# One matmul over 128 columns in place of two over 64, in the products of a linear attention layer

## The chip, the cores and the metric

The kernel runs on one core of one Trainium2 chip. The metric is the device time of one execution in microseconds (us), the median of several runs.

## The reference, cut to what matters

The reference is one transformer block over T = 4096 tokens of width 256. A layer norm (scaled and shifted) feeds a gated delta-rule attention with H = 8 heads and M = 8 modes of memory per head; then a second layer norm feeds a mixture of 8 experts, of which each token takes two. Everything is float32. The attention is the long part, and in it each of the 64 pairs of head and mode carries a 64x64 memory S through the tokens:

```python
def step(S, inp):
    q_t, k_t, v_t, b_g, b_beta = inp
    S = S * jnp.exp(b_g)[..., None, None]
    kv = jnp.einsum('mbhk,mbhkv->mbhv', k_t, S)
    dv = (v_t[None] - kv) * b_beta[..., None]
    S = S + k_t[..., :, None] * dv[..., None, :]
    o_t = jnp.einsum('mbhk,mbhkv->mbhv', q_t, S)
    return (S, o_t)
S0 = jnp.zeros((M, B, H, DK, DV), jnp.float32)
_, ys = jax.lax.scan(step, S0, (qt, kt, vt, gt, bt))
```

Queries and keys are rotated by an angle that depends on the mode, and brought to unit length, before this.

## The kernel before, in words

**Tiles and chunks.** The tokens are cut into 32 tiles of 128, a tile into NC = 4 chunks of C = 32 tokens. The 64 pairs of head and mode are taken in two halves of 32 (hh = 0 and 1), a half as HQ = 8 quads q of four modes of one head; the 128 partitions hold four modes x 32. Within a chunk the recurrence is solved in closed form: Gram products of keys with keys and queries, a 32x32 triangular system for each pair (the solve), and then, chunk after chunk, a read of the memories, corrections, and an update of the memories.

**The four products that the edit touches**, all on TensorE (PE), all f32, with 128 rows and a stationary operand of 128 columns that is cut into SIDES, columns 0 to 63 and 64 to 127, each in a matmul of its own that writes 64 partitions of the result:
- gram(u, c), L518: keys `ke` against keys and queries `kq`, 64 moving columns, for 8 quads and r = 0, 1 (the halves of the key's 64 dimensions).
- memory_read(v, hh, c), L557: `ke` against `state`, 64 moving columns, 8 quads x 2, in two groups g of four quads, each with a semaphore of its own.
- corrections(v, hh, c), L574: `te` (the inverse) against `rhs`, 64 moving columns, 8 quads, in two groups; behind each group stand the half-width products of L580 (`state` against the queries `qg`), which write outputs to 64 partitions at a time.
- update_and_outputs(v, c), L593: `kte` against `dvs`, 64 moving columns, 8 quads x 2, in two groups; behind each stand the half-width products of L601.

The stationary operands `ke`, `te` and `kte` are block-diagonal, with 32x32 blocks for the four modes of a quad; ScalarE (ACT) copies the blocks into place (L751, L758, L793).

**Order.** The order is written out by hand, for each engine in a function half(n, hh), and the engines meet at counting semaphores. In half(n, hh) each engine does the front of its own half u = 2n + hh and, in between, the four chunks of the half before, v = u - 1. On PE: read, corrections, update of chunk 0; read of chunk 1, rows (L493), corrections, update; replicate (L502), read of chunk 2, replicate, corrections, update; rows, read of chunk 3, corrections, gram 0, rows, update of chunk 3, gram 1, 2, 3; then project_out (even halves, L610), values (L529), the next tile's projections (L467), route (even halves, L618 and L623), sum_squares (L475). The read of the next chunk 0 stands at the head of the next half, behind columns (L483) in the even ones, and so runs during the solve.

On VectorE (DVE): right_sides (L1237, L1240) takes a read and makes `rhs`; decayed_corrections (L1247) takes the corrections and makes `dvs`; update_memories (L1256, L1258) adds the update to the state and takes the outputs. Between them stand the front's operations (angles, L1119 to L1127; decays, L1144 to L1148; rotate_keys, L1163 to L1173; chunk_systems, L1205 and L1206, which take a Gram product each; queries_for_memories, L1197). At the end comes the solve, L1210 to L1224, some 31 pairs of short operations, without PE. GpSimd (POOL) fades the state (L1527) between corrections and update, and rotates the queries.

In each group PE waits for DVE's result and DVE for PE's, as here:

```python
pe.wait_ge(sem(f"state_ready{g}"), since(f"state_ready{g}", vc))
pe.wait_ge(sem(f"dv_ready{g}"), since(f"dv_ready{g}", vc))
pe.wait_ge(sem(f"out_taken{g}"), since(f"out_taken{g}", vc))
```

Gram products, rows and key replicas go through two PSUM banks in turn (to_dve); PE waits for a bank to be freed.

Of the kernel before, what the change touches and what calls it, by code (L numbers as in the profile page):

```python
# [21 lines left out]
P = 128  # L22
# [3 lines left out]
H, M, DK = 8, 8, 64  # L26
FR = DK // 2
C = 32
# [3 lines left out]
HQ = Q // 2  # L32
# [87 lines left out]
def build(nc, x_in, Wq, Wk, Wv, Wbeta, Wtg, mode_logits, log_decay, omega_log, Wg, Wo,  # L120
# [11 lines left out]
    with outer, ctx:  # L132
# [35 lines left out]
        def sb(name, shape, dt=F32):  # L168
            return ctx.enter_context(nc.sbuf_tensor(name, shape, dt))
# [6 lines left out]
        bank_mem = banks[4:6]  # L176
        bank_upd = banks[6:8]
# [70 lines left out]
        dvs = sb("dvs", [P, HQ, DK])  # L248
# [5 lines left out]
        kq = sb("kq", [P, 2, HQ, 2, P])  # L254
        ke = sb("ke", [P, NC, 2, HQ, P])
        kte = sb("kte", [P, 2, HQ, P])
        te = sb("te", [P, HQ, P])
# [6 lines left out]
        state = sb("state", [P, Q, 2, DK])  # L264
        rhs = sb("rhs", [P, HQ, DK])
# [148 lines left out]
        def _(pe):  # L414
# [92 lines left out]
            SIDES = (slice(0, 64), slice(64, 128))  # L507

            def gram(u, c):

                pe.wait_ge(sem("q_rotated"), since("q_rotated", u + 1))
                pe.wait_ge(sem("ke_ready"), 4 * u + c + 1)

                def emit(b):
                    for q in range(HQ):
                        for r in range(2):
                            for s in SIDES:
                                mm = pe.matmul(b[s, q * 2 * C:(q + 1) * 2 * C], ke[:, c, r, q, s],  # L518
                                               kq[:, r, q, :, c * C:c * C + C], start=(r == 0), stop=(r == 1))
                    return mm  # L520
                to_dve(emit)

# [24 lines left out]
            def memory_read(v, hh, c):  # L547

                vc = 4 * v + c
                for g in range(2):  # L550
                    pe.wait_ge(sem(f"state_ready{g}"), since(f"state_ready{g}", vc))
                    pe.wait_ge(sem(f"dv_ready{g}"), since(f"dv_ready{g}", vc))
                    pe.wait_ge(sem(f"out_taken{g}"), since(f"out_taken{g}", vc))
                    for q in range(4 * g, 4 * g + 4):
                        for r in range(2):
                            for s in SIDES:
                                mm = pe.matmul(bank_mem[g][s, q % 4 * DK:q % 4 * DK + DK], ke[:, c, r, q, s],  # L557
                                               state[:, hh * HQ + q, r, :], start=(r == 0), stop=(r == 1))
                    mm.then_inc(sem(f"ks_full{g}"), 1)

            def out_bank(g, side):
# [3 lines left out]
            def corrections(v, hh, c):  # L565

                vc = 4 * v + c
                for g in range(2):
                    pe.wait_ge(sem(f"rhs_ready{g}"), since(f"rhs_ready{g}", vc + 1))  # L570
                    pe.wait_ge(sem("te_ready"), vc + 1)
                    for q in range(4 * g, 4 * g + 4):
                        for s in SIDES:
                            pe.matmul(bank_mem[g][s, q % 4 * DK:q % 4 * DK + DK], te[:, q, s], rhs[:, q, :], start=True, stop=True)  # L574
                    pe.wait_ge(sem("qg_ready"), v + 1)
                    for j in range(2):
                        for r in range(2):
                            for side in range(2):
                                q = 4 * g + 2 * side + j
                                mm = pe.matmul(out_bank(g, side), state[:, hh * HQ + q, r, :], qg[:, r, q, c * C:c * C + C],  # L580
                                               start=(j == 0 and r == 0), stop=False)
                    mm.then_inc(sem(f"dv_full{g}"), 1)

            def update_and_outputs(v, c):

                vc = 4 * v + c
                for g in range(2):
                    pe.wait_ge(sem(f"dvs_ready{g}"), since(f"dvs_ready{g}", vc + 1))
                    pe.wait_ge(sem("kte_ready"), vc + 1)
                    for q in range(4 * g, 4 * g + 4):  # L590
                        for r in range(2):
                            for s in SIDES:
                                mm = pe.matmul(bank_upd[g][s, (q % 4) * P + r * DK:(q % 4) * P + r * DK + DK],  # L593
                                               kte[:, r, q, s], dvs[:, q, :], start=True, stop=True)
                    mm.then_inc(sem(f"upd_full{g}"), 1)
                    pe.wait_ge(sem(f"dv_ready{g}"), since(f"dv_ready{g}", vc + 1))
                    pe.wait_ge(sem("pw_ready"), since("pw_ready", v + 1))
                    for j in range(2):
                        for side in range(2):
                            q = 4 * g + 2 * side + j  # L600
                            mm = pe.matmul(out_bank(g, side), dv[:, q, :], pw[:, c, q, :], start=False, stop=(j == 1))  # L601
                    mm.then_inc(sem(f"out_full{g}"), 1)
# [1207 lines left out]
```

## Time and profile before

| | |
|---|---|
| time, median of 3 runs | 7432.92 us (7431.34 to 7433.24) |
| the profiled execution's own time | 7433.18 us |
| its span, first to last instruction | 7431.5 us |
| mean granted TensorE clock | 0.803 |
| busy: PE, PEld, DVE, ACT, POOL | 61%, 53%, 77%, 44%, 44% of the span |

Busy time is the time in which an engine had at least one instruction under way. PE is the matmul side of TensorE, PEld its weight loads, which overlap it.
### The profile page before, as it was taken

What the parts mean: (1) busy time and instruction counts of PE and PEld (TensorE: products, weight loads), DVE (VectorE), ACT (ScalarE), POOL (GpSimd) and SP (SyncE); (2) the same over time, 40 slices, a digit from 0 to 9 for tenths busy, and PEclk for the clock granted to TensorE, in tenths of its full rate; (3) what the DMA queues carried; (4) which work ended last, traced back from release to release, by engine and by line L of the source; (5) the groups of instructions that cost most, each with busy time, mean ns of one, the idle gap of its engine ahead of it and who ended that gap; (6) DMA issues with size and microseconds to landing.
All of it is one profiled execution on the core that took longest, in us unless ns stands there. A gap on an engine that the chain in (4) does not pass through costs nothing. (4 is left out here: it accounts for less than half of the span.)

```text
span 7431.5 us, 196282 instructions
## 1 busy us (share of the span) xinstructions
PE 4567.1 (61%) x78513; PEld 3915.4 (53%) x78513; DVE 5741.0 (77%) x10216; ACT 3284.2 (44%) x5497; POOL 3289.4 (44%) x2021
## 2 busy tenths in 40 slices
PE   1565656656666666566565666666665656663994
PEld 0455555555555555555555555555555555553662
DVE  5788888888888888888888888888888888883003
ACT  0444445444445444454444544444444445452220
POOL 0545454454454454544545544445445455453003
PEclk9787778877778777787777887777877778876997
DMA  2000000000000000000000000000000000003223
GB/s 80 1 5 5 5 5 5 3 4 5 5 5 5 5 5 5 5 5 2 5 5 5 5 5 5 5 5 5 5 2 5 5 5 5 5 4 108 68 71 99
DMA packets 68598, 107.85 MB, mean 15 GB/s; under 512 B 11824, under 2 KB 57200, under 8 KB 66544
## 3 DMA queue, kind: packets, MB, share of 16 engines
q1 hardware_dynamic: 59248, 69.78, 2.9%
q0 software_dynamic: 8448, 25.18, 1.1%
q8 instruction: 672, 11.01, 0.6%
q14 instruction: 230, 1.88, 0.1%
HBM read 57.32 MB, written 37.62 MB: 13 GB/s over the span
## 5 line engine op out<-in xcount | busy, mean ns | idle before, releaser
L1527 POOL TENSOR_TENSOR state<-state,gc_end 128x512 f32<-128x512 f32 x512 | 594.9, 1174 | 1359.2 <-PE bank L580 1319.0
L574 PE MATMUL bank<-rhs,te 128*64 128x64 f32 x8192 | 451.8, 270 | 887.4 <-DVE rhs L1240 551.3
L574 PEld LDWEIGHTS bank<-rhs,te 128*64 128x64 f32 x8192 | 378.1, 177 | 974.1 <-DVE rhs L1240 925.5
L557 PE MATMUL bank<-state,ke 128*64 128x64 f32 x16384 | 660.3, 249 | 319.3 <-DVE outT L1258 232.2
L557 PEld LDWEIGHTS bank<-state,ke 128*64 128x64 f32 x16384 | 620.9, 161 | 439.9 <-DVE state L1256 247.7
L751 ACT ACTIVATE te<-tt 32x256 f32<-32x256 f32 x1024 | 421.9, 412 | 742.8 <-DVE tt L1224 732.3
L593 PE MATMUL last_two<-dvs,kte 128*64 128x64 f32 x16384 | 638.2, 236 | 180.5 <-DVE dvs L1247 180.5
L1221 DVE TENSOR_TENSOR last_two<-last_two,prod 128x31 f32<-128x31 f32 (+15 forms) x1984 | 692.6, 349 | 68.1
L793 ACT ACTIVATE ke<-kq 32x512 f32<-32x512 f32 x1024 | 642.7, 628 | 201.7 <-DVE kq L1173 188.0
L1219 DVE TENSOR_TENSOR prod<-bd,last_two 128x31 f32<-128x31 f32 (+15 forms) x1984 | 671.1, 338 | 71.9
L593 PEld LDWEIGHTS last_two<-dvs,kte 128*64 128x64 f32 x16384 | 575.3, 149 | 196.7 <-DVE dvs L1247 187.7
L758 ACT ACTIVATE kte<-kt 32x512 f32<-32x512 f32 x1024 | 641.5, 626 | 34.4 <-PE last_two L593 21.2
L518 PE MATMUL bank<-kq,ke 128*64 128x64 f32 x16384 | 581.1, 237 | 114.4 <-DVE pw L1206 105.8
L1552 POOL TENSOR_TENSOR pw<-pw,w_quad 128x1024 f32<-128x1024 f32 x64 | 122.4, 1913 | 1176.1 <-DVEq L1398 1176.1
L518 PEld LDWEIGHTS bank<-kq,ke 128*64 128x64 f32 x16384 | 561.5, 152 | 122.6 <-DVE pw L1206 74.7
L1489 POOL TENSOR_TENSOR kq<-tmp,turn 128x1024 f32<-128x1024 f32 x320 | 607.1, 1897 | 32.0 <-POOL pw L1552 5.6
L766 ACT ACTIVATE dv<-bank 128x256 f32<-128x256 f32 x512 | 188.4, 380 | 743.0 <-DVE dvs L1247 733.5
L493 PE MATMUL bank<-row_group,select 128*128 128x128 f32 x3072 | 426.9, 293 | 36.2 <-DVE col L1136 27.6
L1256 DVE TENSOR_TENSOR state<-last_two,state 128x512 f32<-128x512 f32 x512 | 354.0, 691 | 117.4 <-POOL state L1527 77.8
L1722 DVE TENSOR_TENSOR yrow<-last_two,b_row 128x256 f32<-128x256 f32 x64 | 27.2, 425 | 504.5 <-PE last_two L1676 504.5
L493 PEld LDWEIGHTS bank<-row_group,select 128*128 128x128 f32 x3072 | 384.2, 201 | 55.1 <-DVE col L1136 27.9
L1540 POOL TENSOR_TENSOR tmp<-raw,cos_t 128x1024 f32<-128x1024 f32 x64 | 151.8, 2371 | 588.8 <-ACTq L834 588.8
(248 smaller groups left out, 11015.0 us busy)
## 6 DMA issues: line engine op xcount, KB each, us to landing
w_sb<-in_L_ffn_W_dram SPq DMA_DIRECT2D x16, 1024.0 KB, 9.3
expert_rows<-ke SPq DMA_DIRECT2D x1, 8192.0 KB, 21.3
xrows<-expert_rows SPq DMA_DIRECT2D x16, 512.0 KB, 8.3
expert_outputs<-yrow POOLq DMA_DIRECT2D x16, 512.0 KB, 3.4
xt<-_attn_hidden_states_dram SPq DMA_DIRECT2D x32, 128.0 KB, 2.1
xr<-_attn_hidden_states_dram SPq DMA_DIRECT2D x32, 128.0 KB, 2.1
x_after_attention<-xr SPq DMA_DIRECT2D x32, 128.0 KB, 1.7
xo<-x_after_attention SPq DMA_DIRECT2D x32, 128.0 KB, 3.7
```

Source lines behind the costliest of these rows:

```text
L493: mm = pe.matmul(b[:, ql * P:ql * P + P], select[:, b4 * 4 + ql, :], row_group[:, group, :], start=True, stop=True)
L518: mm = pe.matmul(b[s, q * 2 * C:(q + 1) * 2 * C], ke[:, c, r, q, s], kq[:, r, q, :, c * C:c * C + C], start=(r == 0), stop=(r == 1))
L557: mm = pe.matmul(bank_mem[g][s, q % 4 * DK:q % 4 * DK + DK], ke[:, c, r, q, s], state[:, hh * HQ + q, r, :], start=(r == 0), stop=(r == 1))
L574: pe.matmul(bank_mem[g][s, q % 4 * DK:q % 4 * DK + DK], te[:, q, s], rhs[:, q, :], start=True, stop=True)
L593: mm = pe.matmul(bank_upd[g][s, (q % 4) * P + r * DK:(q % 4) * P + r * DK + DK], kte[:, r, q, s], dvs[:, q, :], start=True, stop=True)
L751: ins = act.activation(te[s, :, 32 * m:32 * m + 32], tt[s, c, :, :], ACT.Copy)
L758: ins = act.activation(kte[s, :, :, 32 * m:32 * m + 32].rearrange("p r q f -> p (r q) f"), kt[s, :, :, c * C:c * C + C].rearrange("p r q f ...
L793: ins = act.activation(ke[s, c, :, :, 32 * m:32 * m + 32].rearrange("p r q j -> p (r q) j"), kq[s, :, :, 0, c * C:c * C + C].rearrange("p ...
L1219: ln(dve.tensor_tensor(pr, a_prob[:, j + 1:C, j:j + 1].broadcast_to([P, rows, cols]), t_prob[:, j:j + 1, 0:cols].broadcast_to([P, rows, co ...
L1221: ln(dve.tensor_tensor(below, below, pr, ALU.subtract))
L1489: ln(pool.tensor_tensor(low2 if i else into, part, over_t(table), ALU.mult))
L1527: pool.tensor_tensor(sv, sv, gc_end[:, vh, 4 * g:4 * g + 4, c].unsqueeze(2).broadcast_to([P, 4, 2 * DK]), ALU.mult).then_inc(sem(f"state_f ...
```

## The change

In the four products the loop over SIDES goes, and one matmul takes all 128 stationary columns and writes all 128 partitions of the result. The moving operand, the order, the waits and the semaphores stay. The products of L580 and L601 stay as they are, 64 columns at a time.

```diff
                 def emit(b):
                     for q in range(HQ):
                         for r in range(2):
-                            for s in SIDES:
-                                mm = pe.matmul(b[s, q * 2 * C:(q + 1) * 2 * C], ke[:, c, r, q, s],
-                                               kq[:, r, q, :, c * C:c * C + C], start=(r == 0), stop=(r == 1))
+                            mm = pe.matmul(b[:, q * 2 * C:(q + 1) * 2 * C], ke[:, c, r, q, :],
+                                           kq[:, r, q, :, c * C:c * C + C], start=(r == 0), stop=(r == 1))
...
                         for r in range(2):
-                            for s in SIDES:
-                                mm = pe.matmul(bank_mem[g][s, q % 4 * DK:q % 4 * DK + DK], ke[:, c, r, q, s],
-                                               state[:, hh * HQ + q, r, :], start=(r == 0), stop=(r == 1))
+                            mm = pe.matmul(bank_mem[g][:, q % 4 * DK:q % 4 * DK + DK], ke[:, c, r, q, :],
+                                           state[:, hh * HQ + q, r, :], start=(r == 0), stop=(r == 1))
...
                     for q in range(4 * g, 4 * g + 4):
-                        for s in SIDES:
-                            pe.matmul(bank_mem[g][s, q % 4 * DK:q % 4 * DK + DK], te[:, q, s], rhs[:, q, :], start=True, stop=True)
+                        pe.matmul(bank_mem[g][:, q % 4 * DK:q % 4 * DK + DK], te[:, q, :], rhs[:, q, :], start=True, stop=True)
...
                         for r in range(2):
-                            for s in SIDES:
-                                mm = pe.matmul(bank_upd[g][s, (q % 4) * P + r * DK:(q % 4) * P + r * DK + DK],
-                                               kte[:, r, q, s], dvs[:, q, :], start=True, stop=True)
+                            mm = pe.matmul(bank_upd[g][:, (q % 4) * P + r * DK:(q % 4) * P + r * DK + DK],
+                                           kte[:, r, q, :], dvs[:, q, :], start=True, stop=True)
```

## Rows read from the trace of the kernel before

**Rows 1.** Page: busy share of each engine, and PE's granted clock in 40 slices.
```profile
PE 4567.1 (61%) x78513; PEld 3915.4 (53%) x78513; DVE 5741.0 (77%) x10216; ACT 3284.2 (44%) x5497; POOL 3289.4 (44%) x2021
...
PEclk9787778877778777787777887777877778876997
```

**Rows 2.** Windows: stretch, length, busy us of each engine, PEclk, DMA share, GB/s.
```profile
3055.00:3059.70 4.70, 2.85 (x54) 2.88 (x56) 4.04 (x7) 1.77 (x5) 0.74 (x1) 0.50 0.02 3
3059.70:3069.00 9.30, 7.08 (x179) 6.77 (x179) 7.86 (x13) 6.79 (x12) 1.36 (x2) 0.99 0.01 2
...
3055.00:3154.50 99.50, 63.29 (x1208) 55.53 (x1208) 83.44 (x152) 50.11 (x85) 47.80 (x26) 0.81 0.03 7
3154.50:3259.80 105.30, 64.57 (x1192) 57.00 (x1192) 89.62 (x156) 48.68 (x82) 50.31 (x32) 0.78 0.01 2
```

**Rows 3.** Timeline, PE: start, us, line, shape, records, idle before and its releaser.
```profile
3041.53 1.92 PE L483 MATMUL bank<-cmat,xg 128*128 128x32 f32 x8 [9.18 <-DVE xg L1090]
3043.37 3.34 PE L557 MATMUL bank<-state,ke 128*64 128x64 f32 x64
3056.85 1.12 PE L574 MATMUL bank<-rhs,te 128*64 128x64 f32 x16 [10.14 <-ACT te L751]
3057.73 1.05 PE L580 MATMUL bank<-qg,state 128*64 128x32 f32 x16
3058.55 1.13 PE L574 MATMUL bank<-rhs,te 128*64 128x64 f32 x16
...
3064.79 2.10 PE L557 MATMUL bank<-state,ke 128*64 128x64 f32 x64 [2.22 <-DVE outT L1258]
3066.82 2.05 PE L493 MATMUL bank<-row_group,select 128*128 128x128 f32 x16
3068.85 0.69 PE L574 MATMUL bank<-rhs,te 128*64 128x64 f32 x16
...
3069.81 0.66 PE L574 MATMUL bank<-rhs,te 128*64 128x64 f32 x16
...
3070.74 1.13 PE L593 MATMUL last_two<-dvs,kte 128*64 128x64 f32 x32
3071.80 0.42 PE L601 MATMUL bank<-pw,dv 128*64 128x32 f32 x8
...
3101.79 3.15 PE L518 MATMUL bank<-kq,ke 128*64 128x64 f32 x64
...
3124.57 1.95 PE L467 MATMUL bank<-hT,wqk_sb 128*128 128x128 f32 x16
3126.36 0.27 PE L618 MATMUL bank<-cmat,xn 128*128 128x128 f32 x1
...
3128.47 0.61 PE L623 MATMUL bank<-wr_sb,h2T 128*128 128x8 f32 x4 [0.93 <-ACTq L883]
```

**Rows 4.** Timeline, DVE, in the same columns.
```profile
3018.32 0.17 DVE L1077 RECIPROCAL stat<-stat 128x1 f32<-128x1 f32 x1 [2.22 <-ACT stat L773]
...
3071.03 0.42 DVE L1247 TENSOR_TENSOR dvs<-bank,dec_end 128x256 f32<-128x256 f32 x1 [0.51 <-PE bank L580]
...
3078.80 0.42 DVE L1237 TENSOR_TENSOR rhs<-bank,eg_col 128x256 f32<-128x256 f32 x1
...
3079.88 1.23 DVE L1163 TENSOR_TENSOR tmp<-bank,cos_t 128x1024 f32<-128x1024 f32 x1 [0.19 <-DVE rhs L1240]
...
3091.60 0.69 DVE L1256 TENSOR_TENSOR state<-last_two,state 128x512 f32<-128x512 f32 x1 [1.04 <-POOL state L1527]
...
3104.99 0.42 DVE L1205 TENSOR_TENSOR cos_t<-bank,bd 128x256 f32<-128x256 f32 x1 [1.40 <-PE bank L518]
...
3119.84 0.42 DVE L1206 TENSOR_TENSOR pw<-bank,dec 128x256 f32<-128x256 f32 x1
```

**Rows 5.** Groups by line: shape, records, busy us, mean ns, idle before, releasers.
```profile
L557 PE MATMUL bank<-state,ke 128*64 128x64 f32 x16384 | 660.3, 249 | 319.3 <-DVE outT L1258 232.2 <-issue 87.1
...
L574 PE MATMUL bank<-rhs,te 128*64 128x64 f32 x8192 | 451.8, 270 | 887.4 <-DVE rhs L1240 551.3 <-ACT te L751 336.0
```

## The prediction

> **What bounds the kernel now.** I read the page's busy shares first, then the windows with the granted clock, then the timelines of PE and DVE over one half tile side by side, and the groups by line last, for counts. The page says DVE 77% and PE 61% busy [rows 1], which reads as a DVE-bound kernel with room on PE. The windows keep that picture and give the period: a pair of halves takes 99.5 + 105.3 = 204.8 us, with PE busy 63 to 65 us and DVE 83 to 90 us of each half [rows 2]. The timelines correct it. From the end of the solve (3055) to the last Gram product (3120) DVE and PE work in a ring: DVE waits for each read, correction, update and Gram product, and PE waits for the DVE operation between them [rows 3, 4]. From 3064.8 to 3073 PE runs without a gap: read of chunk 1, rows, corrections, update. There every added PE microsecond lands on the path. The solve, where PE idles ten microseconds on end (ahead of 3056.85), hides what is added there (the read of chunk 0).
>
> **Price of one record.** An f32 matmul is two records here: 16,384 records at L557 are 8,192 half matmuls [rows 5]. So are they at L518 and L593, and 8,192 records at L574 are 4,096. The edit turns 57,344 half-width records into 28,672 full-width ones, 448 for each half tile (read 128, corrections 64, update 128, Gram 128). Full clock, half width: 64 records of L557 start at 3064.79 and the next line at 3066.82, 0.032 us each, 0.062 to 0.064 a pair (16 of L574 in 0.52 give 0.065) [rows 3]. Full clock, full width: 16 records of L467 (128 moving columns) take 1.79, 0.112 each. With fewer moving columns it gets no cheaper: the four of L623 stream 8 columns and take 0.61 in all; less the length of a single one (0.27, the L618 row) that is 0.34 for three starts, 0.113. So a full-width record costs what its 128 stationary columns cost, and 64 moving columns stream under it. Half clock: L483 (32 moving columns, full width) takes 1.84 for 8 with one turn behind, 0.215 each; a pair of halves takes 2 x 0.055 = 0.11 (16 of L574 in 0.88) [rows 3]. A merged record thus costs 0.112 in place of 0.063, or 0.215 in place of 0.11. Bounds where no row shows 64 columns on 128: below, the stream alone, half of L467's 0.112 = 0.056; above, 0.127 (16 of L493 in 2.03). I take 0.112, since 8 and 128 columns cost the same.
>
> The Trainium skill, page "TensorE: Matmul & The Clock Gate", speaks for both. Its section "Back-to-back issue gap" gives about 60 cycles for anything up to 64 moving columns; by that a merged record would take about 0.025 to 0.05 us and PE would get lighter. Its section "LDWEIGHTS (loading the stationary operand)" has the time go by stationary columns, 128 / 1.2 GHz, an estimate of 0.107. The L623 row sides with the second.
>
> **Turns.** The output products of L580 and L601 stay half width, so PE now turns between full and half width inside every chunk: eight times. The 16 records of L493 take 2.03 where 16 x 0.112 = 1.79, with a turn on either side: about 0.1 us a turn, between 0 and 0.24 [rows 3].
>
> **New stage costs, full clock.** Read of a chunk: 32 x 0.112 = 3.6 for 2.0. Corrections: a group takes 0.96 (3068.85 to 3069.81); its 16 half records (0.5) become 8 x 0.112 = 0.9 and two turns 0.2, so 1.55, twice. Update: a group of 32 half records (1.06, from 3070.74 to 3071.80) and 8 of L601 at 0.03 becomes 1.8 + 0.2 + 0.2 = 2.2, twice. Gram: 3.6 for 2.0. Removing instructions frees nothing else: PE's queue order, all waits and all DMAs stay.
>
> **The clock.** The half starts with PE at half clock after ten idle microseconds (3055 to 3059.7 at 0.50), and it rises at 3059.8, after 3 us of closely packed half-width work [rows 2, 3]. With merged records at half clock the same columns stream over twice the time (0.215 for 0.11), so the array is half as densely fed. The L483 work, thin and full width, ran at the half clock throughout. I therefore take it that the clock stays low through chunk 0 and the read of chunk 1 and rises only in the rows products of L493, whose 128 moving columns feed the array fully. Once up I let it stay up while PE is not kept waiting, as in 3059.7 to 3069 (0.99). No row here shows a packed but thin burst, so that the clock rises as early as now is the first rival. The Trainium skill, page "TensorE: Matmul & The Clock Gate", section "What's actually happening", ties the clock to how busy PE has been; a merged burst has no gaps, so that reading speaks for this rival.
>
> **The sum along one half** (times of the half that starts at 3055; delay against it) [rows 3, 4].
> Chunk 0 at half clock: corrections 2 x (8 x 0.215 + 0.82 for L580 + 0.24) = 5.5 from 3056.85, to 3062.3; update 2 x (3.4 + 0.34 + 0.24) = 8.0, to 3070.3; read of chunk 1, 32 x 0.215 = 6.9, to 3077.2; rows, mostly at half clock, 3.1, to 3080.3. Corrections of chunk 1 began at 3068.85: +11.5. DVE's work in between (add, columns, state, sin_t, unit: about 7 us) lies beside this.
> Chunk 1 at full clock: corrections +1.1, so DVE's second dvs (3071.03) is 12.5 late; update +1.8, read of chunk 2 +1.5, with a few tenths of turns: the rhs of 3078.80 is +15.4.
> Chunk 2: the update was waited for by nobody: DVE rotates keys from 3079.9 on and then waits for POOL's fade at 3091.60. Eight microseconds of update, if the 2 us gap ahead of it drops the clock again, just fit beneath: 0 (at most 1.2).
> Chunk 3: that update runs from 3100.6 to 3108.0, the rows behind it to 3111.1, the read to 3114.7. Its second rhs is then ready at 3115.9, 0.5 more than 15.4 late; the second group of corrections ends at 3117.8 and the first Gram product (3101.79 now) at 3121.3. DVE, which waits 1.40 for it at 3104.99, takes it at 3121.6: +16.6.
> Update of chunk 3 and Gram products 1 to 3: DVE had 2.0 us of its own work between products that took 2.0; now they take 3.6, PE sets the pace, and the last product (3119.84) is +19.0.
> Behind it, project_out is late by 0.7 in the even halves; in the odd ones ACT's square root is queued behind the values products, and DVE's wait of 2.22 for it (3018.32) grows by 2.5.
> That is 19.7 + 21.5 = 41.2 us a tile. There are 63 halves with memories, 31.5 tiles: 1,298. The four chunks after the last half have no rows products among them and run at half clock: by the same prices about 30 (10 to 60). The first half adds 3. Together 1,330 on the profiled execution's own 7433.18 (span 7431.5; the median of the runs is 7432.92, so the two need no correction): 8,760.
>
> **Rivals.**
> First, the clock rises as early as now. Then chunk 0 costs 0.9, the read 1.6 and the corrections 1.1, less 0.4 of turns that the rows no longer need: +3.2 at 3071.03. Update and read make +6.3 at 3078.80, the first Gram product +6.8 at 3104.99, update and three Gram products +9.2 at 3119.84. With the same two extras as above that is 9.9 and 11.7 a half, 21.6 x 31.5 + 15 = 695: 8,130. For it: PE is packed in chunk 0 as before. Against: the thin stream at half clock, above. Chance 0.20.
> Second, the clock stays low for longer: the rows products don't lift it, and chunk 1 and the first Gram product run at half clock too: corrections 5.5 for 3.1, update 8.0 for 4.4, read 6.9 for 3.6, Gram 6.9 for 3.6, some 12.6 more a half, about 9,550. Against: those rows products stream twice the columns per record. Chance 0.08.
> Third, on the other side: the stationary load hides behind the stream, the lower bound of 0.056 holds. Then a half's 448 records save 448 x (0.063 - 0.056) = 3 us, and some 21 more turns at 0.1 cost 2: no change, 7,420 to 7,445. It decides in favour of the change only if a turn is free, too. The one thing for it is that no row has 64 moving columns on 128; L623 speaks against it. Chance 0.05, in equal parts above and below the mark.
> Fourth, that the added PE time vanishes in PE's 36 us of idle a half (7,433). That idle is in one long gap in the solve and in gaps at which PE waits for a DVE result that itself waits for PE. I give it 0.01.
>
> **How the numbers follow.** My forecast has 0.66; its own range, from the turn (0 to 0.24), the update of chunk 2 (0 to 1.2) and the point in the rows where the clock rises (plus or minus 2 us a half), is 8,600 to 8,920. To hold 8 in 10 the range takes in the first rival: 8,100 to 9,000. About 0.2% is what a measurement tells from no change here; slower by more than that 0.94, within it 0.03, faster 0.03.
>
> **What would show it.** In the profile after: records of L518, L557, L574 and L593 halved, start to start 0.11 at full clock (0.056 would make the third rival right); the window from the end of the solve to the read of chunk 1 at a granted clock near 0.5 (near 1.0 from 5 us on is the first rival); DVE's idle time ahead of L1237, L1247, L1256 and L1205 grown to some 20 us a half; a pair of halves near 246 us, DVE's busy time unchanged. A pair under 210 us would make the forecast wrong at its root.

## The result, and the profile after: slower by a fifth

The median after is 8904.3 us (8895.3 to 8907.9, 4 runs) against 7432.8 (7431.3 to 7433.2, 4 runs): a ratio of 1.198, 95% interval [1.196, 1.200], or +1,471 us. The prediction was 8,760 in a range of 8,100 to 9,000, so direction and mechanism held, and the growth of 1,330 was 140 us (10%) short; two larger errors lie beneath it and partly cancel, as the part on the prediction shows. Lines behind the change moved up by four, so that L1247 of before is L1243 of after; the merged products are L517 (Gram), L555 (read), L571 (corrections) and L589 (update), and the half-width ones L577 and L597. In the experiments further on the lines shift again by a few, and the names of the tiles tell which product a row is.

The page of the kernel after, busy us of each engine and the granted clock in 40 slices:

```profile
PE 7003.8 (79%) x49841; PEld 6362.6 (71%) x49841; DVE 5544.0 (62%) x10216; ACT 3299.5 (37%) x5497; POOL 3270.1 (37%) x2021
...
PEclk9677777777777777777777777777777777776797
```

Against [rows 1] PE has 28,672 fewer records, as counted, and 2,437 us more of busy time; the mean granted clock fell from 0.803 to 0.748. The half tile that stood at 3055 in [rows 2 to 4] stands at 3666.5 now (subtract 611.5 to compare). Windows of it, in the columns of [rows 2]:

```profile
3666.66:3671.20 4.54, 2.82 (x24) 2.72 (x24) 3.62 (x6) 1.54 (x4) 0.00 (x0) 0.50 0.00 0
3671.20:3683.00 11.80, 11.80 (x79) 11.21 (x75) 5.33 (x9) 3.37 (x8) 2.10 (x2) 0.50 0.00 0
3683.00:3689.90 6.90, 6.90 (x33) 6.90 (x34) 2.98 (x6) 6.00 (x7) 0.00 (x0) 0.50 0.01 2
3689.90:3705.50 15.60, 14.83 (x135) 13.09 (x133) 6.27 (x14) 4.81 (x10) 2.10 (x2) 0.90 0.01 1
...
3713.70:3729.80 16.10, 16.10 (x96) 15.74 (x96) 9.59 (x13) 9.81 (x18) 13.83 (x7) 0.58 0.01 2
3729.80:3743.30 13.50, 13.47 (x148) 12.85 (x146) 8.87 (x15) 5.79 (x10) 2.10 (x2) 1.00 0.00 1
```

PE is busy without a gap from 3671.2 to 3689.9, and its clock stays at the lower level (0.50) all that time, where before it rose after 4.7 us [rows 2]. The timeline of PE, in the columns of [rows 3]:

```profile
3668.38 1.94 PE L571 MATMUL bank<-rhs,te 128*128 128x64 f32 x8 [6.52 <-ACT te L747]
...
3674.15 3.68 PE L589 MATMUL last_two<-dvs,kte 128*128 128x64 f32 x16
...
3682.51 7.09 PE L555 MATMUL bank<-state,ke 128*128 128x64 f32 x32
3689.39 3.73 PE L493 MATMUL bank<-row_group,select 128*128 128x128 f32 x16
3692.91 1.05 PE L571 MATMUL bank<-rhs,te 128*128 128x64 f32 x8
...
3713.70 3.68 PE L589 MATMUL last_two<-dvs,kte 128*128 128x64 f32 x16 [1.67 <-DVE dvs L1243]
...
3722.06 3.78 PE L493 MATMUL bank<-row_group,select 128*128 128x128 f32 x16
3725.64 4.40 PE L555 MATMUL bank<-state,ke 128*128 128x64 f32 x32
...
3733.07 3.79 PE L517 MATMUL bank<-kq,ke 128*128 128x64 f32 x32
```

Start to start, a full-width record takes 0.213 us at half clock (the median of such distances; 32 of L555, and the next line starts 6.88 later) and 0.112 at full (32 of L517, next start at 3736.70). The rows products at 3689.39 still take 3.52 to the next start, so the clock rose only at their end; by the trace's clock records it did so at 3693.0. DVE on the other side of the ring:

```profile
3674.34 0.42 DVE L1243 TENSOR_TENSOR dvs<-bank,dec_end 128x256 f32<-128x256 f32 x1 [2.54 <-PE bank L577]
...
3682.10 0.69 DVE L1252 TENSOR_TENSOR state<-last_two,state 128x512 f32<-128x512 f32 x1 [3.26 <-PE last_two L589]
...
3689.71 0.42 DVE L1233 TENSOR_TENSOR rhs<-bank,eg_col 128x256 f32<-128x256 f32 x1 [2.60 <-PE bank L555]
...
3696.29 0.42 DVE L1243 TENSOR_TENSOR dvs<-bank,dec_end 128x256 f32<-128x256 f32 x1 [1.20 <-PE bank L577]
...
3707.32 0.42 DVE L1233 TENSOR_TENSOR rhs<-bank,eg_col 128x256 f32<-128x256 f32 x1 [0.97 <-PE bank L555]
...
3724.18 0.69 DVE L1177 TENSOR_TENSOR bd<-bank,dec 128x512 f32<-128x512 f32 x1 [0.98 <-PE bank L493]
...
3736.90 0.42 DVE L1201 TENSOR_TENSOR cos_t<-bank,bd 128x256 f32<-128x256 f32 x1 [2.29 <-PE bank L517]
...
3754.72 0.42 DVE L1202 TENSOR_TENSOR pw<-bank,dec 128x256 f32<-128x256 f32 x1
```

Every wait in these rows names PE, with a product of the ring behind it. Summed over the kernel, DVE's groups by line show where the time sits. First the kernel before, then after; the last figures are the idle time ahead of the group:

```profile
L1237 DVE TENSOR_TENSOR rhs<-bank,eg_col 128x256 f32<-128x256 f32 x512 | 217.4, 425 | 202.8 <-issue 98.5 <-PE bank L557 69.5 <-DVE tt L1224 1.0
L1247 DVE TENSOR_TENSOR dvs<-bank,dec_end 128x256 f32<-128x256 f32 x512 | 217.3, 424 | 113.1 <-PE bank L580 96.7
L1256 DVE TENSOR_TENSOR state<-last_two,state 128x512 f32<-128x512 f32 x512 | 354.0, 691 | 117.4 <-POOL state L1527 77.8 <-DVE qg L1198 14.4 <-DVE tmp L1124 6.8
L1205 DVE TENSOR_TENSOR cos_t<-bank,bd 128x256 f32<-128x256 f32 x256 | 108.7, 425 | 111.9 <-PE bank L518 89.0
L1181 DVE TENSOR_TENSOR bd<-bank,dec 128x512 f32<-128x512 f32 x128 | 88.5, 691 | 15.4
```

```profile
L1233 DVE TENSOR_TENSOR rhs<-bank,eg_col 128x256 f32<-128x256 f32 x512 | 217.3, 424 | 635.1 <-PE bank L555 528.8 <-issue 98.7 <-DVE tt L1220 1.0
L1243 DVE TENSOR_TENSOR dvs<-bank,dec_end 128x256 f32<-128x256 f32 x512 | 217.2, 424 | 550.1 <-PE bank L577 537.7
L1252 DVE TENSOR_TENSOR state<-last_two,state 128x512 f32<-128x512 f32 x512 | 353.9, 691 | 564.8 <-PE last_two L589 485.1 <-POOL state L1523 65.5 <-DVE qg L1194 14.2
L1201 DVE TENSOR_TENSOR cos_t<-bank,bd 128x256 f32<-128x256 f32 x256 | 108.7, 425 | 270.7 <-PE bank L517 266.9
L1177 DVE TENSOR_TENSOR bd<-bank,dec 128x512 f32<-128x512 f32 x128 | 88.5, 692 | 99.8 <-PE bank L493 99.7
```

The idle time ahead of these five grew by 432 + 437 + 447 + 159 + 84 = 1,560 us. DVE's own busy time fell by 197 (5741.0 to 5544.0), so that 1,363 of the 1,471 stand in these rows; 86 more are the odd halves' wait for ACT's square root (2.8 a half), and 24 the even halves' wait for project_out.

### The profile page after: what moved, and what is told of

The parts are those of the page before. It is cut to its first block and busy times, and to the rows that moved or that the text cites. A ratio compares the mean times of both kernels' runs of the same rounds, so it can differ in the third digit from the quotient of the medians.

```text
span 8901.4 us, 138938 instructions
## 1 busy us (share of the span) xinstructions
PE 7003.8 (79%) x49841; PEld 6362.6 (71%) x49841; DVE 5544.0 (62%) x10216; ACT 3299.5 (37%) x5497; POOL 3270.1 (37%) x2021
## 5 line engine op out<-in xcount | busy, mean ns | idle before, releaser
L589 PE MATMUL last_two<-dvs,kte 128*128 128x64 f32 x8192 | 1444.5, 350 | 110.8 <-DVE dvs L1243 110.8
L555 PEld LDWEIGHTS bank<-state,ke 128*128 128x128 f32 x8192 | 1381.2, 266 | 142.5 <-issue 138.2
L589 PEld LDWEIGHTS last_two<-dvs,kte 128*128 128x128 f32 x8192 | 1367.8, 261 | 138.3 <-DVE dvs L1243 118.0
L555 PE MATMUL bank<-state,ke 128*128 128x64 f32 x8192 | 1397.3, 351 | 59.7 <-issue 59.7
L571 PE MATMUL bank<-rhs,te 128*128 128x64 f32 x4096 | 683.2, 322 | 502.7 <-DVE rhs L1236 284.1
L571 PEld LDWEIGHTS bank<-rhs,te 128*128 128x128 f32 x4096 | 632.3, 234 | 555.9 <-DVE rhs L1236 513.5
L517 PE MATMUL bank<-kq,ke 128*128 128x64 f32 x8192 | 945.5, 276 | 7.7 <-POOL kq L1543 7.7
L517 PEld LDWEIGHTS bank<-kq,ke 128*128 128x128 f32 x8192 | 927.9, 192 | 13.5 <-POOL kq L1543 8.0
L1233 DVE TENSOR_TENSOR rhs<-bank,eg_col 128x256 f32<-128x256 f32 x512 | 217.3, 424 | 635.1 <-PE bank L555 528.8
L1243 DVE TENSOR_TENSOR dvs<-bank,dec_end 128x256 f32<-128x256 f32 x512 | 217.2, 424 | 550.1 <-PE bank L577 537.7
```

Source lines behind the costliest of these rows:

```text
L517: mm = pe.matmul(b[:, q * 2 * C:(q + 1) * 2 * C], ke[:, c, r, q, :], kq[:, r, q, :, c * C:c * C + C], start=(r == 0), stop=(r == 1))
L555: mm = pe.matmul(bank_mem[g][:, q % 4 * DK:q % 4 * DK + DK], ke[:, c, r, q, :], state[:, hh * HQ + q, r, :], start=(r == 0), stop=(r == 1))
L571: pe.matmul(bank_mem[g][:, q % 4 * DK:q % 4 * DK + DK], te[:, q, :], rhs[:, q, :], start=True, stop=True)
L589: mm = pe.matmul(bank_upd[g][:, (q % 4) * P + r * DK:(q % 4) * P + r * DK + DK], kte[:, r, q, :], dvs[:, q, :], start=True, stop=True)
```

## The experiments

### One of the four products at a time

Each run takes one of the four hunks of the change and leaves the other three products in halves.

```diff
 e1_gram_only   +  mm = pe.matmul(b[:, ...], ke[:, c, r, q, :], kq[...], ...)
 e2_read_only   +  mm = pe.matmul(bank_mem[g][:, ...], ke[:, c, r, q, :], state[...], ...)
 e3_corr_only   +  pe.matmul(bank_mem[g][:, ...], te[:, q, :], rhs[:, q, :], ...)
 e4_upd_only    +  mm = pe.matmul(bank_upd[g][:, ...], kte[:, r, q, :], dvs[:, q, :], ...)
```

Gram products: 

> Only the Gram products (L518) are merged to 128 columns; reads, corrections and updates stay in halves. Theory (a full-width record costs what its 128 stationary columns cost, and a thin merged burst does not lift the clock): the first Gram product starts at half clock now (3101.79), so it costs 6.8 for 2.9 us and the rows behind it some 1 more; products 1 to 3 cost 2.4 behind the update; with project_out and ACT's square root some 1.6: about 8.5 us a half, 7,900 to 8,000 us. Rival, that only the price of the record counts and the clock goes as before: 1.6 + 2.4 + 1.6 = 5.6 a half, about 7,790. Rival, that the load hides behind the stream: 7,430.

Read: 

> Only the reads (L557) are merged. Theory: reads of chunks 1 and 2 cost 1.6 each at full clock and land on the path, the read of chunk 3 falls partly at half clock and is partly covered by DVE, the read of chunk 0 lies in the solve: 3 to 4.5 us a half, 7,620 to 7,720 us. Rival, that the load hides behind the stream: 7,430.

Corrections: 

> Only the corrections (L574) are merged, which brings a turn to and from half width around each group. Theory: +1.2 us a chunk at full clock and some 2 at half clock; chunk 2 is covered by DVE's rotation; the clock rises one step later in chunk 0: about 4 us a half, 7,630 to 7,730 us. If a turn costs nothing: 2.5 us a half, about 7,590. Rival, that the load hides behind the stream and only the turns are left: about 7,460.

Update: 

> Only the updates (L593) are merged. Theory: +1.8 to 2 us in each of chunks 0, 1 and 3 at full clock, more where the burst meets the half clock (odd halves, chunk 0), chunk 2 mostly covered: 5.5 to 8 us a half, 7,780 to 7,930 us. The four parts then add up to about the 1,471 us of the whole; a sum well below it would say that the merged kernel pays for something that no part alone brings (the longer stretch at half clock). Rival, that the load hides behind the stream: 7,440.

| alone | median us | ratio to before | growth |
|---|---|---|---|
| Gram | 7869.5 | 1.059 [1.057, 1.061] | 437 |
| read | 7808.7 | 1.051 [1.050, 1.053] | 376 |
| corrections | 7754.8 | 1.044 [1.042, 1.045] | 322 |
| update | 7755.3 | 1.044 [1.042, 1.045] | 322 |

No part is free, and together they make 1,457, which is the whole within 1%. That sum is no proof that the parts are independent: the update alone takes 71 us off DVE's wait for the Gram products (111.9 before, 40.8 then). In size all four expectations were off, Gram and update below their range, read and corrections above. For Gram, the first product of a half meets half clock and a waiting DVE:

```profile
2960.28 7.09 PE L517 MATMUL bank<-kq,ke 128*128 128x64 f32 x32
...
2967.41 0.42 DVE L1204 TENSOR_TENSOR cos_t<-bank,bd 128x256 f32<-128x256 f32 x1 [5.46 <-PE bank L517]
```

```profile
L1204 DVE TENSOR_TENSOR cos_t<-bank,bd 128x256 f32<-128x256 f32 x256 | 108.7, 425 | 442.1 <-PE bank L517 434.2
```

That wait was 1.40 [rows 4], so 4.1 us a half (3.9 expected), or some 260 us. Over the kernel DVE's idle time ahead of all four Gram products grew by 330 us (442.1 for 111.9), which leaves some 70 for products 1 to 3, 1.1 a half for the 2.4 expected. The rows that the queries wait for add 52, the square root in the odd halves (5.01 for 2.22 in [rows 4]) 86 and project_out 24, all near what was expected; and DVE's own busy time fell by 59. So Gram came under its range by products 1 to 3 and by DVE's shorter operations.

Update alone, DVE's idle time ahead of the state additions grew by 320 us and ahead of bd by 84; 71 less at the Gram products and 89 less of busy time gave part of it back. Corrections alone, the waits grew by 2.3 us a half in chunk 0, 1.3 in chunk 1 and 1.4 ahead of the Gram products, each a little over its price. The read shows a cost of another kind. The read of chunk 1 stands behind a gap (2.10 here), and in 47 of 63 halves the clock falls within it, although the corrections and updates before it are still in halves (4.66 us to the next start here, 3.59 in the other halves). It takes the rows products behind it along:

```profile
3001.46 4.86 PE L556 MATMUL bank<-state,ke 128*128 128x64 f32 x32 [2.10 <-DVE outT L1257]
3006.12 3.73 PE L493 MATMUL bank<-row_group,select 128*128 128x128 f32 x16
```

DVE then waited 4.11 us for the corrections (0.38 before), and 1.85 in the halves in which the clock stayed up. So the price of a merged product includes the clock of work behind it that the change doesn't touch.

### The price of a record, by itself

Blocks of matmuls on constants, placed ahead of the first tile, each on a line of its own; the rest is the kernel before. It leaves nothing out.

```diff
+            for _ in range(60):
+                pe.matmul(bank_mem[1][:, 0:64], ident, cmat[:, 0:64], start=True, stop=True)
+            for _ in range(100):
+                for s in SIDES:
+                    pe.matmul(bank_mem[1][s, 0:64], ident[:, s], cmat[:, 0:64], start=True, stop=True)
...
```

> The kernel before with ten blocks of matmuls of constants put ahead of its first tile, one line each, so its time is not compared. Full width with 64 moving columns (60 matmuls), half-width pairs of 64 (100), full width 64 (120), full width 32 (80), 128 (60), 256 (60), pairs of 32 (80), full 128 (60), full 8 (60), full 128 (30). Theory: start to start of a full-width record is 0.112 us at full clock and 0.213 at half for 8, 32, 64 and 128 moving columns alike, 0.216 for 256; a pair of half-width records of 64 is 0.06. The first block, thin and packed, leaves the clock at half although PE never pauses; the pairs lift it; the second block of 64 keeps it; the block of 32 loses it. Rival on the clock (it goes by packed or not): the first block lifts it within a few us and nothing loses it. Rival on the price: 64 and 32 moving columns cost 0.056 and less.

The timeline of PE over the blocks:

```profile
153.68 25.83 PE L435 MATMUL bank<-cmat 128*128 128x64 f32 x120 [116.37 <-POOLq L1483]
179.44 13.35 PE L438 MATMUL bank<-cmat 128*64 128x64 f32 x400
192.72 27.01 PE L440 MATMUL bank<-cmat 128*128 128x64 f32 x240
219.57 30.54 PE L442 MATMUL bank<-cmat 128*128 128x32 f32 x160
...
265.53 26.07 PE L446 MATMUL bank<-cmat 128*128 128x256 f32 x120
291.53 9.53 PE L449 MATMUL bank<-cmat 128*64 128x32 f32 x320
300.98 13.66 PE L451 MATMUL bank<-cmat 128*128 128x128 f32 x120
314.49 21.27 PE L453 MATMUL bank<-cmat 128*128 128x8 f32 x120
```

Three things can be read. First, 240 full-width records with 64 moving columns take 26.85 us to the next start, 0.112 each; with 128 columns it is 0.113 (L451), and with 8 columns (L453) the records stand 0.112 apart as well, until the clock falls in it, too. Only with 256 does the stream show (0.216). A half-width record takes a quarter of 0.112: once L438 is at full clock its records stand 29 ns apart on average, 58 ns a pair, and with 32 moving columns (L449) it is 30 ns. So the price goes by the stationary side up to 128 moving columns, and two stationary operands of 64 columns side by side cost half of one of 128. (Two on the same side in a row were not run.) The prediction's third rival needed 0.056 for the merged record.

The Trainium skill's page "TensorE: Matmul & The Clock Gate" has in its section "Back-to-back issue gap" a table with some 60 cycles for up to 64 moving columns. The table is for an isolated matmul, and the section says that in a stream of weight loads and matmuls both set the spacing; the 0.112 of this stream agrees with the text and not with the table. The section "LDWEIGHTS (loading the stationary operand)" takes columns / 1.2 ns, which makes an estimate of 107 ns for 128 columns, near the 112 measured at full clock. It makes 53 ns for 64 columns, where this stream has 29, and it doesn't tell the two levels of the clock apart, where this stream has 213 at the lower one.

Second, PE has no gap in L435 and yet its records stand 0.215 us apart for 25.8 us, the price at half clock. The trace has no clock record ahead of the first rise, which comes 3.3 us into the half-width pairs of L438, so the view prints 1.00 for this stretch and the half clock is inferred from the distances; a DMA load of 205 GB/s runs beside L435, too, and it is the less clean of the two witnesses. Third, a thin stream even loses the clock. The window in L442, whose records have 32 moving columns:

```profile
223.70:249.90 26.20, 26.20 (x125) 26.20 (x125) 0.00 (x0) 0.00 (x0) 0.00 (x0) 0.50 0.00 1
```

PE is busy for 26.20 of 26.20 us and its clock is at the lower level. With 64 columns (L440) it kept the upper level; L435 did not reach it. The same page of the Trainium skill, section "What's actually happening", lets the clock follow how busy PE has been; by busy time as the profile counts it this window should have kept the clock, and it didn't.

### How much of the loss is clock

First, chunk 0 and the read of chunk 1 go back to halves, and all else stays merged:

```diff
+                            for s in (SIDES if c == 1 else (slice(0, P),)):    # read
...
+                        for s in (SIDES if c == 0 else (slice(0, P),)):        # corrections, update
```

> The changed kernel with the corrections and update of chunk 0 and the read of chunk 1 in halves again, three of its fifteen stages. Theory: the clock rises in chunk 0 as in the kernel before, and the 13.7 us by which DVE is late at the corrections of chunk 1 shrink to about 2 (rows and corrections): 11 to 12 us a half, about 8,180 us. Rival (only the price at full clock counts): the three stages give back 0.9 + 1.6 and little more, about 3 us a half, 8,710.

Measured: 8189.3 us, ratio 1.102 [1.100, 1.104]. With 80 of a half's 448 merged records (corrections 16, update 32, read 32) split again, 715 of 1,471 us are gone. At the record's full-clock price they would be 80 x 0.05 = 4 us a half, some 250, and six turns fewer at 0.1 some 40; the rest is the clock, which rises in chunk 0 again.

Second, the records stay merged, and PE gets full matmuls of 512 moving columns, their result unused, in its idle time ahead of the corrections of chunk 0:

```diff
+            def fill(n):
+                if n:
+                    b = to_scalar.bank()
+                    pe.wait_ge(sem(f"act_bank_free{b}"), since(f"act_bank_free{b}", to_scalar.uses_of_bank()))
+                    for _ in range(n):
+                        pe.matmul(bank_act[b][:, :], ident, cmat[:, 0:512], start=True, stop=True)
...
                     memory_read(v, vh, 0)
+                    fill(5 if hh == 0 else 8)
                     corrections(v, vh, 0)
```

> The changed kernel with full-width matmuls of constants, 512 moving columns each, put into PE's gap between the read of chunk 0 and its corrections (5 in the even halves, 8 in the odd ones; results are not used). No stage of the change is touched; only PE's clock at the start of the ring differs. Theory: corrections 3.2 for 5.8, update 4.6 for 8.4, read 3.6 for 6.9, rows 1.8 for 3.5, that is 11.4 us of PE, of which about 10.5 reach the path: 63 x 10.5 = 660, about 8,240 us. If the clock has no part in it: 8,904 or more.

Measured: 8280.0 us (8250.2 to 8367.1), 1.117 [1.111, 1.123]: 624 us less for added work. In the profiled execution the clock fell again in chunk 0 in 11 of the 32 odd halves, which then took 126.8 us in place of 117.5 or 119.3; so the 624 are what these fillers gave, not the whole of what the clock costs. Then one matmul more, ahead of the update of chunk 2, which in the kernel after starts behind a wait of 1.67 and runs at half clock:

```diff
                     corrections(v, vh, 2)
+                    fill(1)
                     update_and_outputs(v, 2)
```

> The changed kernel with the filler of chunk 0 and one filler more ahead of the update of chunk 2, PE's next gap (1.67 us). Theory: that update, the rows behind it and the start of the read of chunk 3 come at full clock, and DVE's waits there (0.8 for the update, 1.0 and 1.0 for rows, 1.7 and 1.0 for the read) mostly go: 4 to 5 us a half, about 8,000 us. What then is left over 7,433 is the price at full clock, 9 us a half. If the clock costs nothing there: 8,280.

A miss: 8680.5 us (8665.7 to 8684.6), 1.168 [1.166, 1.170], 400 us worse than without it. It did what it was put there for: the update of chunk 2 and the read of chunk 3 ran at full clock. But the fall only came later, in the thin, waiting work of chunk 3, where the first Gram product sits:

```profile
3262.57 1.10 PE L579 MATMUL bank<-rhs,te 128*128 128x64 f32 x8 [1.14 <-DVE rhs L1246]
...
3265.06 1.97 PE L579 MATMUL bank<-rhs,te 128*128 128x64 f32 x8 [0.80 <-DVE rhs L1246]
...
3267.96 7.09 PE L525 MATMUL bank<-kq,ke 128*128 128x64 f32 x32
```

The half lengths became 122 in place of 108.6 in the even halves and 120 to 121 in place of 117.5 to 126.8 in the odd ones. The last experiment takes that up, with fillers at every thin place (6 and 10 at chunk 0, and two each ahead of the update of chunk 2, the read and the corrections of chunk 3):

```diff
+                    fill(6 if hh == 0 else 10)
                     corrections(v, vh, 0)
...
+                    fill(2)
                     update_and_outputs(v, 2)
                 rows(2 + hh)
                 if not first:
+                    fill(2)
                     memory_read(v, vh, 3)
+                    fill(2)
                     corrections(v, vh, 3)
```

> The changed kernel with extra full matmuls (512 moving columns, result unused) ahead of the corrections of chunk 0 (6 and 10 a half), and two each ahead of the update of chunk 2, the read of chunk 3 and its corrections, where one filler at chunk 2 alone had only moved the place at which the clock falls. If what is left beyond the merged records' own price is the clock, and thin stages need company at every gap, then all stages run at full clock: the price is that of the prediction's first rival, 21.6 us a tile or some 680 us, on the 7,381 of the unchanged kernel with the same fillers: 8,030 to 8,150, halves of some 105 and 117, the first Gram product streaming 32 records in 3.8. If the thin full-width stages lose the clock whatever stands between them, 8,300 to 8,700 as in the two versions with fewer fillers, with updates of 3.68 a group in chunk 2 or a Gram 0 of 7.09.

Measured: 8119.6 us (8117.7 to 8121.9), 1.092 [1.091, 1.094], halves of 108.1 and 117.2. Of the 8,192 full-width records each of the update and of Gram products, 2% at most ran at half clock; what else did is the read of chunk 0, beneath the solve. The page's clock slices, and the read of chunk 1 and Gram product 0 that took 7.09 in the kernels above:

```profile
PEclk9798888988889888898888998889888899886997
```

```profile
3007.83 3.79 PE L563 MATMUL bank<-state,ke 128*128 128x64 f32 x32
...
3050.64 3.79 PE L525 MATMUL bank<-kq,ke 128*128 128x64 f32 x32
```

So of the 1,471 us, 785 go away when fillers hold the clock, and 687 are what the merged records and turns cost at full clock (with what the fillers cost or give themselves). The split depends on what it is measured against: the kernel before gains 52 us by fillers in the same places (below), and between the two kernels with fillers 738 us are left. The first rival of the prediction (8,130) had about this price, though not quite this course: it let the clock rise only in chunk 0, after 3 us, and here it is up before chunk 0 begins.

### The same fillers on the kernel before

If the clock is worth that much, the kernel before may gain too. It got fillers ahead of chunk 0 alone (9 and 10), at the late places alone (2, 2, 2), and at both.

```diff
+                    fill(9 if hh == 0 else 10)
                     corrections(v, vh, 0)
```

Chunk 0 alone: 

> The kernel before with the same filler ahead of the corrections of chunk 0 (9 in the even halves, 10 in the odd). Theory: corrections and update of chunk 0 run at full clock, DVE's second dvs comes 0.85 us earlier and in the odd halves the update too: 1 to 1.5 us a half, about 7,350 us. Rival, that fillers run into the corrections and delay them: 7,440 to 7,500.

Late places alone: 

> The same with the fillers of chunks 2 and 3 alone. If the two places are independent and the half clock in chunk 3 costs about 1.1 us of DVE's time a half: 7,360 to 7,380. If DVE's work covers PE there: 7,430.

Both: 

> The kernel before with fillers ahead of the corrections of chunk 0 (9 and 10) and two more each ahead of the update of chunk 2, of the read of chunk 3 and of the corrections of chunk 3, so that chunk 3 and the first Gram product run at full clock too. The filler at chunk 0 alone gained 0.85 us by chunk 1 and lost it again in front of the first Gram product, where DVE waits 1.84 in place of 1.41. If that loss is the half clock in chunk 3, DVE's wait there shrinks by some 1.1 and the gain of chunk 0 is kept: up to 2 us a half, 7,300 to 7,350. If the fillers themselves delay the read and corrections behind them: 7,430 to 7,500.

| fillers | median us | ratio to before |
|---|---|---|
| chunk 0 | 7433.8 | 1.0002 [0.9993, 1.0011] |
| late places | 7403.9 | 0.996 [0.995, 0.998] |
| both | 7381.2 | 0.993 [0.992, 0.994] |

All three came out slower than expected, late places by 24 us and both by 31 above their ranges. Chunk 0 alone was a miss by 80 us, and it is the instructive one. The granted clock rose from 0.803 to 0.849, DVE's idle time ahead of the dvs group fell by 34 us, and the time did not move. Part of it was given back at the first Gram product:

```profile
L1256 DVE TENSOR_TENSOR dvs<-bank,dec_end 128x256 f32<-128x256 f32 x512 | 217.4, 425 | 79.5 <-PE bank L588 61.0
...
L1214 DVE TENSOR_TENSOR cos_t<-bank,bd 128x256 f32<-128x256 f32 x256 | 108.8, 425 | 130.2 <-PE bank L526 107.2
```

Against 113.1 and 111.9 before, 34 us are won and 18 lost in these two lines, and DVE's own busy time grew by 14 (5755.1 for 5741.0), 17 of it in one operation on two SBUF operands (`tmp` from `tmp` and `cos_t`): together that is nothing. By halves, from solve to solve, the kernel won 0.24 us in the even ones (97.04 for 97.28) and lost 0.24 in the odd ones (107.76 for 107.52); the wait for the first product grew in both, in an even half to 1.84 from 1.40. Why that product comes later was not traced further. With fillers at the late places too, the wait for the Gram products falls to 66.2 us and the kernel is 0.7% faster than the kernel before, a small gain against an expected 1 to 2%. The late places alone give 0.4%.

## Why the prediction was right, and where it was short

**The bound.** The ring of DVE and PE was the limit, not DVE's busy share. PE had 39% idle time before, 2,864 us, and it took up two fifths of the added work: PE's busy time grew by 2,437 us, its idle time fell by 967, and the span grew by 1,470. What fell into idle time lies where the prediction had put it at nothing, the read of chunk 0 beneath the solve (7.07 us for 3.34) and the update of chunk 2 beneath DVE's key rotation; the rest is on the ring.

**Price of one record.** Predicted 0.112 and 0.215; measured 0.112 and 0.213. The four records of L623 with 8 moving columns [rows 3] were the right witness.

**Turns.** Predicted 0.1 us. Full to half width is 0.205 in place of 0.112 at full clock, so 0.09; half to full is 0.152 in place of 0.03 to 0.05, so 0.10 to 0.12. At half clock they cost more, 0.14 (0.350 for 0.213) and about 0.12. The prediction had 0.24 for two, for 0.26 measured.

**The clock.** Predicted to stay low through chunk 0 and the read of chunk 1 and to rise in the rows products. It rose at the end of these, so they cost 3.52 rather than 3.1; over all halves it rose between 0.8 us before their end and 1.3 behind it.

**The sum along one half.** Delay against the same point of the kernel before. The shown half is that of [rows 3, 4] (start after, less 611.52, less start before); it is one of 9 even halves of 31 that took 121.3 us where the others took 120.3, so the medians of all even and all odd halves stand beside it, counted from the first `rhs` of the half.

| landmark | predicted | shown half | even halves | odd halves |
|---|---|---|---|---|
| corrections of chunk 1 | 11.5 | 12.5 | 12.5 | 12.5 |
| second dvs of chunk 1 | 12.5 | 13.7 | 14.1 | 13.9 |
| second rhs of chunk 2 | 15.4 | 17.0 | 17.4 | 17.1 |
| first Gram product taken | 16.6 | 20.4 | 19.3 | 19.8 |
| last Gram product taken | 19.0 | 23.4 | 22.3 | 21.5 |
| whole half | 19.7 even, 21.5 odd | 24.1 | 23.1 | 22.4 |

So a pair of halves grew by 45.4 us and not by 41.2, to 250.2, which makes 132 of the missing 140. The first half (4 us for 3) and the end (31 for 30) were as predicted. The mis-sized terms are several:
- Up to chunk 1, 1.4 to 1.6 us: from the first corrections of chunk 0 to those of chunk 1 PE took 24.5 us for 23.5 (corrections 5.8 for 5.5, update 8.4 for 8.0, rows 3.5 for 3.1), and in half of all halves the clock rose only within the corrections of chunk 1.
- Chunk 1 to chunk 2, 0.3: the prediction's own terms, 12.5 + 1.8 + 1.5, make 15.8, and it wrote 15.4 without a reason for the difference. 3.3 was measured, as its two terms have it.
- Chunk 2 to the first Gram product: 1.2 predicted, 1.9 and 2.7 measured, 3.4 in the shown half. The prediction had the late update (3100.6 to 3108 of the old times) hide beneath key rotation and fade, and had the rows products cost 3.1 behind it. It hides, nearly: DVE waited 0.78 for its second group. But DVE also needs those rows products, for bd (L1177), before it takes the read of chunk 3. The prediction followed only the read and the rhs behind them. So DVE waits 0.98 and 1.02 there and 1.7 and 1.0 at the next rhs, and the clock, down again since the 1.67 us wait, rises only within the read (4.24 us to the next start where 3.6 was taken). The line's idle time of 99.8 us for 15.4 says the same over the whole kernel.
- Behind the last Gram product the even halves cost 0.8 for 0.7. In the odd ones the wait for the square root grew by 2.8 (2.5 predicted), but the half by only 0.9, since DVE's own operations there became 1.9 us shorter.

The last point holds for the whole kernel, and it is luck. DVE's idle time grew by 1,667 us, a quarter more than the 1,330 predicted, and its busy time, which the prediction had unchanged, fell by 197. Part of that, 1.6 to 2.0 us a half, fell between chunk 2 and the first Gram product, where the waits alone grew by 3.5 and 4.5 us and not by 1.2. With DVE's busy time as predicted, the kernel would have come out near 9,100 if every wait had stayed, above the stated range; that is an estimate, 8,904 + 197, and no run shows it.

**The rivals.** The first (the clock rises as early as now, 8,130) is not what this kernel does, but its price is near that of the version with fillers throughout, 8,120. The second failed with the rows products, at whose end the clock is up again. The third failed with 0.112. Of the fourth, that the added time vanishes in PE's idle, two fifths came true and 1,470 us did not.

## What to carry to other kernels

Two half-width matmuls side by side are not overhead to be merged away when the moving operand is narrow: in f32 a pair of half-width records took 58 to 59 ns with 32 or 64 moving columns, and a merged record 112 with 8 to 128. With 256 columns the stream sets the pace (0.216); whether merging pays there no run here shows. Where DVE and PE wait for each other, PE's 39% of idle time is slack only for what lies outside the ring, and a stage's clock belongs to its price: look at the granted clock in the window of each stage, and count the work behind it that slows down as well. Fillers in PE's idle time can hold the clock, but in these runs one of them moved its fall to a dearer place (8,280 to 8,681), and only with every thin stage covered was it gone (8,120).

## What was not expected

DVE's busy time was predicted to stay and fell by 197 us. Of it 82 are in one line, `rhs` from `v_sb` and `rhs`, both in SBUF (L1240 before, L1236 after). Minimum, median and maximum of its 512 instances:

```profile
L1240 DVE TENSOR_TENSOR rhs<-v_sb,rhs x512: 424/426/2004, 288.3 to 6770.0; 128x256 f32<-128x256 f32 x171
```

```profile
L1236 DVE TENSOR_TENSOR rhs<-v_sb,rhs x512: 424/425/1087, 292.5 to 8238.8; 128x256 f32<-128x256 f32 x171
```

Split by what POOL does meanwhile, the 380 instances before without a POOL instruction beside them take 425 ns on average, and the 132 with one take 1194 ns (68 of them stay below 0.5 us, and the other 64 take 2.0 on average); after, only 31 have one beside them, at 1068 ns. With its waits for PE in between, DVE meets POOL less often here. The Trainium skill, page "GPSIMD Engine Reference", section "1. Specifications", calls POOL's SBUF interface shared with VectorE where VectorE has two SBUF inputs; this split agrees with it, but no run here takes POOL's work away, so that the cause is argued and not shown.

And the granted clock alone doesn't tell the time: the kernel before with fillers at chunk 0 had 0.849 for 0.803 and the same time.
